# Linear attention, 16 batches: the orders of ScalarE, GpSimd and SyncE, and both ends of the program, rewritten

## What is computed

```python
xn = groupnorm(x)                                  # 32 groups, per batch
q, k, v = split(xn.T @ qkv_w.T + qkv_b)
k = relu(k + pos_enc);  q = relu(q)
z = 1.0 / (einsum('bic,bc->bi', q, k.sum(axis=1)) + 1e-06)
kv = einsum('bjc,bjd->bcd', k, v)
out = einsum('bic,bcd,bi->bid', q, kv, z)
y = x + (out @ proj_w.T + proj_b).T
```

## Time and profile before

| | |
|---|---|
| median of 3 runs | 2761.89 us (2757.27 to 2762.05) |
| the profiled execution, its own time | 2772.32 us |
| its span, first to last instruction | 2770.5 us |
| TensorE matmul busy | 2625.4 us, 95% |
| GpSimd busy | 1929.7 us, 70% |
| ScalarE busy | 1664.1 us, 60% |
| VectorE busy | 1610.3 us, 58% |
| DMA moved | 642.07 MB, mean 232 GB/s |
| mean granted TensorE clock | 0.988 |

### The profile page before, as it was taken

The page is one execution under the profiler, slowest core; times in us unless marked ns, Lnnn a source line. Parts: engine busy times, 40 slices in busy tenths (PEclk is TensorE's granted clock), DMA queues, the critical chain, the costliest instruction groups (busy, mean ns, idle before and its releaser), DMA issues.

```text
span 2770.5 us, 45261 instructions
## 1 busy us (share of the span) xinstructions
PE 2625.4 (95%) x15812; PEld 2230.1 (80%) x15812; DVE 1610.3 (58%) x2525; ACT 1664.1 (60%) x2544; POOL 1929.7 (70%) x1192
## 2 busy tenths in 40 slices
PE   4779999999999999999999999999999999999985
PEld 3667878888887888878888887888888788888864
DVE  5555656656565566656666565565656566655443
ACT  3556656566565656666666665656656566665632
POOL 2436868687676877868687776867768686876842
PEclk9999999999999999999999999999999999999997
DMA  6446878788787887878788787868868787876756
GB/s 223 141 127 196 271 221 259 227 255 252 226 260 222 267 251 225 262 218 263 228 259 262 228 258 225 267 219 259 259 215 263 227 252 234 257 218 202 220 166 183
DMA packets 357471, 642.07 MB, mean 232 GB/s; under 512 B 34432, under 2 KB 55808, under 8 KB 357248
## 3 DMA queue, kind: packets, MB, share of 16 engines
q1 hardware_dynamic: 357248, 639.18, 74.3%
HBM read 519.25 MB, written 119.80 MB: 231 GB/s over the span
## 4 chain that ended last, share of the span: by engine, by line
PE 72%; DVE 10%; ACT 6%; issue 6%; POOL 3%; DMA 2%; SPq 1%; ACTq 0%; DVEq 0%; POOLq 0%
PE psK L514 17%; PE psX L536 15%; PE psX L567 15%; PE psG L526 10%; PE psG L528 5%; PE psT L505 5%; PE psX L553 3%; ACT xn L961 3%; DVE stats L767 2%; DVE psK L784 2%; DVE kk L789 2%; ACT xt L978 1%; POOL hl L1102 1%; POOL q L1120 1%; DVE zt L839 1%
## 5 line engine op out<-in xcount | busy, mean ns | idle before, releaser
L1116 POOL TENSOR_TENSOR kacc<-kacc,kt 128x512 f32<-128x512 f32 x368 | 478.4, 1300 | 380.5 <-ACT kt L990 378.0
L514 PE MATMUL psK<-wqk,hl 128*128 128x256 f32 x4608 | 651.3, 291 | 16.9 <-POOL hl L1102 16.9
L1102 POOL TENSOR_TENSOR hl<-xn,hl 128x512 fp32r<-128x512 f32 x384 | 497.6, 1318 | 243.2 <-ACT hl L973 243.2
L773 DVE TENSOR_TENSOR xt<-psT,xt 128x512 fp32r<-128x512 f32 x400 | 274.7, 687 | 626.9 <-ACT xt L978 626.8
L526 PE MATMUL psG<-kk,xt 128*128 128x512 f32 x1600 | 588.4, 401 | 21.4 <-DVE kk L789 21.4
L536 PE MATMUL psX<-hl,wqk 128*128 128x512 f32 x2304 | 600.4, 396 | 2.2 <-DVE xr L803 2.2
L514 PEld LDWEIGHTS psK<-wqk,hl 128*128 128x128 f32 x4608 | 580.5, 192 | 22.5 <-POOL hl L1102 22.5
L1120 POOL TENSOR_TENSOR q<-q,zb 128x1024 f32<-128x1024 f32 x192 | 461.5, 2404 | 158.3 <-DMA zb<-z_rows 158.3
L567 PE MATMUL psX<-uhl,mhl 128*128 128x512 f32 (+1 forms) x2364 | 557.7, 385 | 11.7 <-DVE uhl L899 11.7
L983 ACT ACTIVATE kk<-psK 128x512 fp32r<-128x512 f32 x400 | 239.8, 600 | 465.3 <-DVE psK L784 459.9
L567 PEld LDWEIGHTS psX<-uhl,mhl 128*128 128x128 f32 x2364 | 435.2, 189 | 103.0 <-DVE uhl L899 12.5
(11 more groups left out here) (112 smaller groups left out, 2354.8 us busy)
## 6 DMA issues: line engine op xcount, KB each, us to landing
zb<-z_rows SPq DMA_DIRECT2D x768, 128.0 KB, 4.4
posb<-pos_plus_bk SPq DMA_DIRECT2D x375, 256.0 KB, 5.4
xs<-in_x SPq DMA_DIRECT2D x184, 512.0 KB, 5.9
xa<-in_x SPq DMA_DIRECT2D x184, 512.0 KB, 6.0
xr<-in_x SPq DMA_DIRECT2D x184, 512.0 KB, 3.9
y<-xr SPq DMA_DIRECT2D x184, 512.0 KB, 6.7
z_rows<-zt SPq DMA_DIRECT2D x32, 256.0 KB, 5.4
posb<-in_pos SPq DMA_DIRECT2D x25, 256.0 KB, 2.8
```

What stands on the lines that cost most here:

```text
L514: last = mm(psK[:, par(n, h), i * C:(i + 1) * C], hl_of(t)[:, a, c, s:s + P], wqk[:, w, c, C:2 * C], start=(j == 0), stop=(j == len(terms) ...
L1102: g.tensor_tensor(hl_of(t)[:, 1, :, s], xn_of(n, t)[:, :, s], hl_of(t)[:, 0, :, s], ALU.subtract).then_inc(xl_ready, 1)
L1116: g.tensor_tensor(both, both, kt[:, par(n, h), :], ALU.add).then_inc(ks_done, 1)
```

## The change

The diff, cut to its core. First the order of a common step on ScalarE and GpSimd, which holds for batches 1 to 15:

```diff
             def step(n, t):            # ScalarE
+                if first(n) and t < LAST:
+                    first_step(t)
+                    return
...
+                if t == LAST and n + 1 < B:
+                    normalise(n + 1, 0)
+                    xn_high(n + 1, 0)
                 key_high(n, 2 * t)
...
                 key_keep(n, 2 * t)
-                nxt = (n, t + 1) if t < LAST else (n + 1, 0)
-                if nxt[0] < B:
-                    normalise(*nxt)
-                    xn_high(*nxt)
+                if (n, t) == (B - 1, LAST):
+                    return
+                if t < LAST:
+                    normalise(n, t + 1)
+                    xn_high(n, t + 1)
...
                     x_high_t(n, 2 * t + 1)
-                if has_u(n, t):
-                    u_step(n, t)
-                if t < LAST:
                     key_high(n, 2 * t + 1)
                     key_keep(n, 2 * t + 1)
                 if has_q(n, t):
                     save_q(*q_at(n, t), 1, 0)
+                if has_u(n, t):
+                    u_step(n, t)
...
             def step(n, t):            # GpSimd
-                if has_u(n, t):
-                    scale(*u_of(n, t))
+                if first(n) and t < LAST:
+                    pos_add(2 * t + 2)
+                    xn_low(0, t + 1)
+                    key_sum(0, 2 * t)
+                    if t < LAST - 1:
+                        pos_add(2 * t + 3)
+                    key_sum(0, 2 * t + 1)
+                    return
+                if has_out(n, t):
+                    u_low(*out_of(n, t), uhl)
                 key_sum(n, 2 * t)
                 if t < LAST:
                     xn_low(n, t + 1)
...
                 if has_u(n, t):
-                    u_low(*u_of(n, t), uhl)
+                    scale(*u_of(n, t))
                 if t < LAST:
                     key_sum(n, 2 * t + 1)
```

Then the first batch. Its position code gets the key bias on GpSimd (`pos_add`) and not on VectorE; `gn_root(0)` goes ahead of the weight split on ScalarE; ScalarE has an order of its own:

```diff
+            def first_step(t):
+                x_high_t(0, 2 * t)
+                key_high(0, 2 * t)
+                normalise(0, t + 1)
+                x_high_t(0, 2 * t + 1)
+                key_keep(0, 2 * t)
+                xn_high(0, t + 1)
+                if has_q(0, t):
+                    save_q(*q_at(0, t), 0, 2)
+                key_high(0, 2 * t + 1)
+                key_keep(0, 2 * t + 1)
+                if has_q(0, t):
+                    save_q(*q_at(0, t), 1, 0)
...
+            def pos_add(h):
+                s = pos_slot(0, h)
+                both = posb[:, s, :].rearrange("p (i n) -> p i n", i=TILES)
+                pool.wait_ge(pos_landed[s], pos_no(0, h))
+                g.tensor_tensor(both, both, bk_b[:], ALU.add).then_inc(pos_added, 1)
```

```diff
+        u_last_of = [hl[:, 2], hl[:, 3], (xt), (kk), hl[:, 0], hl[:, 1], uhl[:]]
+        z_places = [xn[:, 0], xn[:, 1], kt[:], zb[:, 0], zb[:, 1]]
+        pairs = (psK, banks8[:, 4:6, :])
...
+            store_z(B - 1, 0)
+            for t in range(5):
+                load_z_last(t)
+            store_y(B - 2, LAST - 3)
             store_y(B - 2, LAST - 2)
+            store_z(B - 1, 1)
             load_last(4)
-            store_z(B - 1, 0)
-            load_zb(B - 1, 0)
-            load_zb(B - 1, 1)
+            load_last(5)
             store_y(B - 2, LAST - 1)
-            load_last(5)
+            load_z_last(5)
+            load_last(6)
             store_y(B - 2, LAST)
-            load_last(6)
+            load_z_last(6)
             for t in range(NBLK):
-                if t + 2 == 8:
-                    store_z(B - 1, 1)
-                if t + 2 < NBLK:
-                    load_zb(B - 1, t + 2)
+                if t + 7 < NBLK:
+                    load_z_last(t + 7)
                 store_last(t)
                 if 7 <= t + 5 < LAST:
                     load_last(t + 5)
```

More of the change, by code:

```diff
@@ L105, in build @@
         y_last = [sem(f"y_last{i}") for i in range(8)]
+        z_last = [sem(f"z_last{i}") for i in range(5)]
         x_first = [sem(f"x_first{i}") for i in range(4)]
@@ L421, in step @@
                     next_pos(n, 2 * t + 1)
-                if has_out(n, t):
+                if has_out(n, t) and (n, t) != (B - 1, LAST):
                     store_y(*out_of(n, t))
@@ L558, in output @@
                 k = size(t)
+                mw = mhl_last if n == B - 1 else mhl
                 pe.wait_ge(ul_ready, blk_no(n, t))
@@ L566, in output @@
                     for j, (c, w, a) in enumerate(terms):
[L567 removed]
+                        last = mm(dst, mw[:, w, c, m * P:(m + 1) * P], u[:, a, c, 0:k],
                                   start=(j == 0), stop=(j == len(terms) - 1))
@@ L777, in key_add @@
                 s = pos_slot(n, h)
-                dve.wait_ge(pos_landed[s], pos_no(n, h))
                 if first(n):
-                    both = posb[:, s, :].rearrange("p (i n) -> p i n", i=TILES)
-                    v.tensor_tensor(both, both, bk_b[:], ALU.add).then_inc(pos_added, 1)
                     dve.wait_ge(pos_added, h + 1)
+                else:
+                    dve.wait_ge(pos_landed[s], pos_no(n, h))
                 dve.wait_ge(k_done, half_no(n, h))
@@ L992, in save_q, with save_from @@
             def save_q(n, t, m, bank):
+                save_from(n, t, m, psX[:, bank, 0:size(t)])
+            def save_from(n, t, m, src):
                 if m == 0:
-                    wait(act, ul_ready, blk_no(*q_gone(n, t)))
+                    if (n, t) == (B - 1, LAST - 1):
+                        act.wait_ge(kt_ready, NHB * B)
+                    else:
+                        wait(act, ul_ready, blk_no(*q_gone(n, t)))
                 act.wait_ge(q_done, two_no(n, t, m))
-                a(q_of(n, t)[:, m, :], psX[:, bank, 0:size(t)], ACT.Relu, bias=bq[:, m:m + 1]).then_inc(q_saved, 1)
+                a(q_of(n, t)[:, m, :], src, ACT.Relu, bias=bq[:, m:m + 1]).then_inc(q_saved, 1)
             def u_high(n, t, u, used):
@@ new lines, in u_last @@
+                    a(pairs[t % 2][:, :, 0:size(t)], q_of(n - 1, t), ACT.Copy)
+                    if t == 0:
+                        act.wait_ge(q_done, two_no(n - 1, q2, 1))
+                    elif t == 1:
+                        act.wait_ge(q_done, two_no(n - 1, q1, 1))
+                    elif t in (2, 3):
+                        act.wait_ge(g_done, NHB * n)
+                    elif t < 7:
+                        act.wait_ge(o_done, two_no(n - 2, t + 6, 1))
+                    else:
+                        act.wait_ge(o_done, two_no(n - 1, t - 7, 1))
@@ new lines, in u_last @@
+                    a(u_last_of[t % 7][:, 0, :, 0:size(t)], q_of(n - 1, t), ACT.Copy).then_inc(uh_ready, 1)
+                g_copy(n - 1)
+                save_q(n - 1, q2, 1, 0)
+                save_q(n - 1, q1, 0, 2)
+                z_plus(n - 1, 0, psK[:, 0, :])
+                save_from(n - 1, q1, 1, psK[:, 1, :])
+                act.wait_ge(q_done, two_no(n - 1, q0, 1))
+                for m in range(CC):
+                    save_from(n - 1, q0, m, psX[:, 2, m * HALF:(m + 1) * HALF])
@@ L1149, in _ @@
                 scale(B - 2, t)
-                u_low(B - 2, t, uhl)
+            for t, u in ((LAST - 2, hl[:, 0]), (LAST - 1, hl[:, 1]), (LAST, uhl)):
+                u_low(B - 2, t, u)
             for t in range(NBLK):
-                scale(B - 1, t)
+                scale_last(t)
 def kernel(**inputs):
```

161 lines of the change are left out of this document (104 added, 57 removed).

## The result

The changed kernel takes 2836.61 us (median of 4 runs, 2834.43 to 2839.39), the kernel before 2761.97 (4 runs): 1.027 times as long, 95% interval 1.0254 to 1.029. The forecast was 2838.

What follows compares the result with a forecast made beforehand. TensorE was taken to bound 14 of 16 batches, but not the two ends. Profiled 2772.3 - 46 (start) + 161 (middle) - 39 (end) = 2848 us, 10 less for the median: 2838; range 2765 to 2890.

Steps and rivals of the forecast that it cites:

- The bound, and what the move does: Common step: TensorE fills its 12.10 us; moving `u_step` and `scale` later makes it about 12.94.
- the loop through `xn_low` and scale: Common step: x_high to normalise, GpSimd's `xn_low` and scale, `u_step`, next x_high; 12.94 us, 14.12 with two blocks' statistics.
- Rival (A): Common step: its loop is hidden, TensorE keeps 12.10 us and only the ends count; 2677 us, chance 0.15.
- The seam: Steps 11, 12, 0, 1, 2 between batches: gains and losses mix, +3.3 us a batch, bounds 0 and +5.
- (C): Between batches: group-norm operations, reciprocals and step 12 all sit on the loop; 2867 us, up to 2890, chance 0.12.
- (B): Whole kernel: common-step loop as forecast, steps between batches neutral, both ends at their best; 2773 us, chance 0.12.
- The start: Batch 0 and the step into batch 1: new order and bias adds off VectorE give -46 us, between -49 and -34.
- "TensorE binds": Batch 0: after the reorder and bias move TensorE limits the step, taken as 9.5 us; 9 steps save 33.
- Rival (D): Batch 0: GpSimd becomes the bound through a late position code, so the start gains nothing; 2884 us, chance 0.03.
- The cover for the position code: Batch 0: DMA brings the position code some 3 us before GpSimd's add; without that, each add delays `xn_low` up to 1.3.
- The end: Batch 15 from its last key product: first output at 31.5 us, DMA limits, end at 85; gain 39, bounds 24 and 54.
- The sum: Whole kernel: 2772.3 - 46 + 161 - 39 = 2848 us profiled, 2838 for the median, slower by 2.8%.

Runs made afterwards that it cites:

- e2: The changed kernel with GpSimd's scale alone moved ahead of the key sum and `xn_low`, `u_step` still last: 2728.9 us.
- e3: The changed kernel with `u_step` alone moved back on ScalarE to behind the second x_high, scale still behind `xn_low`: 3254.3 us.
- e4: The changed kernel with scale multiplying only half of the channels in batches 0 to 14: 2748.9 us.
- e5: The changed kernel with the common step's order of before, and batch 0's key bias added on VectorE again: 2684.1 us.
- e7_two_places: The changed kernel with the common step's order of before, and two places, not five, for the broadcast 1/z at the end: 2787.1 us.

## Why the prediction was right, step by step

**The bound, and what the move does.** Right. TensorE had no slack to give in the middle, and the loop through `xn_low` and scale took its place: 12.92 us measured for 12.94, 14.10 for 14.12, 12.55 for 12.56 without statistics. e2, e3 and e4 change the loop in three ways (scale taken out of it by order, a longer way through ScalarE, scale halved), and each gave the step with one block of statistics that the sum gives. The wait sat where it was forecast, at the output block for GpSimd's low part. Rival (A) is out.

**The seam.** The sum was +3.3 a batch, measured 174.04 - 163.66 - 8.3 = +2.1. A batch cost 10.4 and not 11.6; the middle as a whole +150 against +161. (The upper bound of a batch, with +5 for the seam, adds up to 13.3 and not 13.5; nothing hangs on it.) Within the bounds; (C), the seam at its worst, is out, and (B), with a neutral seam and the ends at their best, wasn't needed. Where in the seam the 1.2 us went wasn't taken apart. One term of the walk did shrink: the group-norm operation of 2.32 us took a mean of 1.17 over the 16 batches before (0.16 to 2.32) and 0.22 after; with its neighbours on either side (L754 and L759, now L804 and L809) it is 2.55 for 1.45. Whether they stood on the path isn't shown.

**The start.** -46 forecast to the start of batch 1, and -46.3 measured to the normalise of its block 1 (161.95 us for 208.22); -45.3 to normalise 12 of batch 0. The terms cancel in part: the first normalise came 1.9 us earlier for 1.5, the two steps without queries saved 9.5 for 8.4, the nine after them 31.6 for 33, the step into batch 1 brought 1.0 for 3, and the first step brought 2.3 for which the sum had no term. "TensorE binds" was right for both edits together, but the argument by VectorE's load wasn't: e5 shows that with the adds on VectorE a loop binds, and not TensorE. Rival (D), GpSimd as the bound, didn't happen: the steps with GpSimd's adds are 9.2 to 9.9 us, but for one of 10.8, and TensorE is busy for all of the 70 us from 60 to 130. The cover for the position code was thinner than forecast, though: instead of finding it in place some 3 us ahead, GpSimd's adds waited 7.1 us for its DMA in all, mostly in the first steps.

**The end.** First output 31.95 us after the last key product, forecast 31.5; end after 84.6, forecast 85. DMA binds it as forecast, at 312 GB/s where I had taken 290.

**The sum.** That 2838 came within 1.4 us of 2836.6 is luck. Between the profiled executions the difference was +65.4 us and my sum +76, 10.6 too much, nearly all of it in the middle. I then took 10 us off, as if the changed kernel's profiled execution would stand as far above its median as that of before; it stood 1 us above. The two errors cancelled.

**The add on the slower engine.** The add takes 1.30 us on GpSimd for 0.68 to 0.78 on VectorE. By the Trainium skill (GPSIMD Engine Reference, Engine selection), GpSimd is about twice as slow for such work and VectorE the engine to use; the trace agrees on the price. But moved to the slower engine, the add left a loop and brought normalise 12 forward by 11.5 us (e5), as GpSimd had room: 7.84 us of work in a step of 9.66.

**The meeting of VectorE and GpSimd.** The prediction took the bias adds of batch 0, 0.78 us with GpSimd at work, for a case in which the two don't exclude each other. That reading was wrong: there it was GpSimd's operation that took longer, as the last section shows.

## What to carry to other kernels

When an instruction is moved in one engine's list, follow what is queued behind it until the path comes back to the same engine: such a loop has a length, and if it is longer than the busiest engine's step, it sets the step, though no engine is full. Work it out from start-to-start distances in one step's timeline; for the changed kernel that was good to 0.02 us, and for its variants to 0.04 in steps with one block of statistics, to 0.4 in those without. Where I judged by load and not by loop, as for VectorE in batch 0 and the two places at the end, I was off by more than 8 us and by 73. Judge a change's ends and its middle apart: 85 us won once at the ends don't pay for 10 us lost in each of 15 batches, and the ends with the old order in the middle gave 0.967.

## What the runs showed of the hardware

VectorE's bias add, two operands in SBUF, took 0.68 us at 89.03 and 1.38 at 94.30 in e5_bias_vector, where GpSimd's second key sum ran until about 95.1. It is as if the add had waited for GpSimd's to end. Before the change the first add of a step met GpSimd's `xn_low`, two operations in a row. The add took 0.77 us, and `xn_low` 2.97, where it took 2.52 in block 0 (at 30.83), as the add came only at its end. The lines of the kernel before:

```profile
108.10 2.97 POOL L1102 TENSOR_TENSOR hl<-xn,hl 128x512 fp32r<-128x512 f32 x2 [1.26 <-ACT hl L973]
...
109.15 0.77 DVE L781 TENSOR_TENSOR posb<-posb,mt 128x512 f32<-128x512 f32 x1
```

And the two key sums of e5_bias_vector, beside the second of which the add took 1.38 us:

```profile
92.39 2.74 POOL L1227 TENSOR_TENSOR kacc<-kacc,kt 128x512 f32<-128x512 f32 x2
```

So the meeting showed in both kernels: in one most of it fell on VectorE, in the other on GpSimd. That agrees with the Trainium skill (SBUF — State Buffer, section SBUF: two separate sides), by which the two exclude each other for the whole instruction.

The granted clock fell to 0.66 in the last 165 us of e7_two_places, where outputs of 4.4 to 5.5 us followed gaps of 8 to 13 us; it was 0.93 in the last 53 us of the changed kernel, with gaps under 4. An output takes 2.9 to 3.0 us at a granted clock of 1.00, the higher level of 2.4 GHz; 5.5 is close to twice that, as at the lower level of 1.2 GHz. In these two stretches the slow outputs come behind gaps of 2 us and more.

DMA moved 312 GB/s at a share of 0.97 while loads, stores and broadcasts were mixed; scaled to full share that is 322, where the last stretch of the kernel before gave 298.
